# Linear layer, routed bias and first keys and values as one unrolled pipeline

## What is computed

```python
x = x + (layernorm(x) @ (weight * block_mask).T + bias)          # linear, block-sparse
h = layernorm(x)
scores = softmax(h @ router_weight.T + router_bias)              # 64 experts
top_w, top_i = top_k(scores, 8)
x = x + h * top_w.sum(-1) + dense(top_w, top_i) @ expert_bias    # routed bias
h = layernorm(x)
latent = concat(h @ Wk_down.T, h @ Wv_down.T)                    # 8 heads of 32 each
k, v = k_latent @ Wk_up.T, v_latent @ Wv_up.T                    # latent reshaped across tokens
# then causal attention with 32 query heads over 8 key heads, and a gated feed-forward of 1376
```

## Time and profile before

| | us |
|---|---|
| median of 3 runs | 1753.33 (1752.32 to 1753.48) |
| span of the profiled execution (its own time outside the span is not shown) | 1755.8 |
| PE busy | 1697.3 (97%) |
| DVE busy | 873.7 (50%) |
| ACT busy | 778.8 (44%) |
| POOL busy | 298.6 (17%) |

### The profile page before, as it was taken

The page is one execution under the profiler, slowest core; times in us unless marked ns, Lnnn a source line. Parts: engine busy times, 40 slices in busy tenths (PEclk is TensorE's granted clock), DMA queues, the critical chain, the costliest instruction groups (busy, mean ns, idle before and its releaser), DMA issues. The chain is left out here.

```text
span 1755.8 us, 27483 instructions
## 1 busy us (share of the span) xinstructions
PE 1697.3 (97%) x8546; PEld 1429.9 (81%) x8546; DVE 873.7 (50%) x2683; ACT 778.8 (44%) x2143; POOL 298.6 (17%) x669
## 2 busy tenths in 40 slices
PE   5788999999999999999999999999999899999999
PEld 4667897788888888888888888888888788888887
DVE  7776010555555555555656556556566553323212
ACT  4476434555455455445445536545545432121111
POOL 4611000121131122122113113112222000000000
PEclk9879999999999999999999999999999999999999
DMA  5200325111111101101101101100100231000000
GB/s 159 70 1 1 150 75 220 37 25 37 37 25 37 37 17 44 37 12 48 37 12 48 38 12 36 39 23 16 45 13 19 77 97 43 1 24 0 24 0 24
DMA packets 46996, 74.42 MB, mean 42 GB/s; under 512 B 4576, under 2 KB 23008, under 8 KB 44832
## 3 DMA queue, kind: packets, MB, share of 16 engines
q1 hardware_dynamic: 45984, 72.63, 12.9%
q10 hardware_dynamic: 896, 0.56, 0.1%
HBM read 52.20 MB, written 20.97 MB: 42 GB/s over the span
## 5 line engine op out<-in xcount | busy, mean ns | idle before, releaser
L963 POOL TENSOR_SCALAR prob<-prob,inv_sum 128x128 f32<-128x128 f32 x256 | 98.5, 385 | 829.5 <-DVE inv_sum L1106 829.5
L1201 PE MATMUL ps_q<-h_hi,kv_w_hi 128*128 128x512 f32 x512 | 205.9, 402 | 1.4 <-PEq L758 1.4
L991 ACT ACTIVATE prob<-prob,neg_max 128x128 f32<-128x128 f32 x256 | 100.6, 393 | 238.5 <-DVE neg_max L1101 238.5
L1201 PE MATMUL ps_q<-h_lo,kv_w_hi 128*128 128x512 f32 x512 | 200.3, 391 | 0.0
L1201 PE MATMUL ps_q<-h_hi,kv_w_lo 128*128 128x512 f32 x512 | 200.0, 391 | 0.0
L133 ACT ACTIVATE prob_t_hi<-ps_s 128x512 fp32r<-128x512 f32 x192 | 107.4, 598 | 73.3 <-PE ps_s L1250 73.3
L964 POOL TENSOR_SCALAR prob<-prob,inv_sum 128x256 f32<-128x256 f32 x256 | 136.9, 535 | 0.0
L1086 DVE TENSOR_TENSOR x<-ps_q,x 128x512 f32<-128x512 f32 x128 | 88.2, 689 | 96.7 <-PE ps_q L1279 96.7
L138 DVE TENSOR_TENSOR prob_t_lo<-ps_s,prob_t_hi 128x512 fp32r<-128x512 f32 x192 | 126.2, 685 | 15.1 <-ACT prob_t_hi L133 12.5
L993 ACT ACTIVATE prob<-prob,neg_max 128x256 f32<-128x256 f32 x256 | 127.1, 497 | 0.0
L1470 DVE SCALAR_TENSOR_TENSOR f_act<-f_ps_r,f_scale,f_act 128x512 f32<-128x512 f32 x44 | 33.0, 751 | 185.5 <-PE f_ps_r L1501 184.1
(11 more groups left out here) (184 smaller groups left out, 4251.4 us busy)
## 6 DMA issues: line engine op xcount, KB each, us to landing
k_scratch<-kv_stage SPq DMA_DIRECT2D x32, 256.0 KB, 2.4
v_scratch<-kv_stage SPq DMA_DIRECT2D x32, 256.0 KB, 2.0
w_raw<-in_wq_g SPq DMA_DIRECT2D x8, 1024.0 KB, 4.8
k_raw<-k_scratch SPq DMA_DIRECT2D x32, 256.0 KB, 3.4
v_raw<-v_scratch SPq DMA_DIRECT2D x32, 256.0 KB, 3.8
w_raw<-in_wo_g SPq DMA_DIRECT2D x8, 1024.0 KB, 5.9
x<-in_x SPq DMA_DIRECT2D x16, 256.0 KB, 2.9
out<-x SPq DMA_DIRECT2D x16, 256.0 KB, 2.1
```

The lines of the kernel that those rows point to most:

```text
L963: pool.tensor_scalar(prob[:, b, h, 0:P], prob[:, b, h, 0:P], inv_sum[:, b, h, 0:1], 1.0, ALU.mult, ALU.mult)
L991: act.activation(prob[:, b, h, 0:P], prob[:, b, h, 0:P], ACT.Exp, scale=-1.0, bias=neg_max[:, b, h, 0:1], accum_out=row_sum[:, b, h, 0:1])
L1201: last = pe.matmul(ps_q[:, h % 2, :], wq[a][:, c, h * HEAD:(h + 1) * HEAD], h3[b][:, c, pair * PAIR:(pair + 1) * PAIR], start=(c == 0 and ...
```

## The change

`block_sparse_linear`, `RouterWeights`, `RoutedBias`, `routed_bias_and_keys`, `skewed` are replaced by one function `head` with one block. All engines run the same unrolled sequence of slots i from -3 to 26; tile i is in the linear stage, and tile j = i - 8 in routing. 48 tasks stand in the slots 18 to 26, at three places of a slot, by the table `KV_PLACES`; the other 48 follow. A routing tile now takes four slots (j, j - 1, j - 2, j - 3) instead of ten iterations, with single buffers for h1, h1t and h2. DVE keeps two instructions of a norm (bn_stats, bn_aggr); POOL has three. The low part of the weight pieces and the scaling of x in routing go to POOL. Loads: the mask is first on SP's queue, the linear weight on ACT's; the wait for a weight piece's buffer is now on POOL's work.

```diff
-def skewed(eng, depth, body, first=None, tail=None):
-    for i in range(first):
-        body(i, i % 2, lambda k, i=i: i - k >= 0)
-    with eng.Fori(first // 2, TILES // 2) as j:
-        for par in range(2):
-            body(2 * j + par, par, lambda k: True)
-    for i in range(TILES, TILES + depth):
-        body(i, i % 2, lambda k, i=i: i - k < TILES)
-        if tail:
-            tail(i - TILES)
...
+class TileNorm:
+    def stats(self, dve, src, t):
+        dve.bn_stats(self.bn[:, t % 2, :], src).then_inc(self.bn_done, 1)
+        dve.wait_ge(self.bn_done, t + 1)
+        dve.bn_aggr(self.mv[:, t, :], self.bn[:, t % 2, :]).then_inc(self.mv_done, 1)
+    def power(self, pool, t):
+        pool.wait_ge(self.mv_done, t + 1)
+        pool.tensor_scalar(self.ve[:, t:t + 1], self.mv[:, t, 1:2], EPS, 1.0, ALU.add, ALU.mult).then_inc(self.ve_done, 1)
+        pool.wait_ge(self.ve_done, t + 1)
+        pool.tensor_tensor(self.factors[:, t, 0:1], self.ve[:, t:t + 1], self.half, ALU.pow).then_inc(self.rstd_done, 1)
+        pool.wait_ge(self.rstd_done, t + 1)
+        pool.tensor_scalar(self.factors[:, t, 1:2], self.mv[:, t, 0:1], self.factors[:, t, 0:1], -1.0, ALU.mult, ALU.mult).then_inc(self.factors_done, 1)
+    def activate(self, act, out, src, t):
+        act.wait_ge(self.factors_done, t + 1)
+        return act.activation(out, src, ACT.Identity, bias=self.factors[:, t, 1:2], scale=self.factors[:, t, 0:1])
...
-                block_sparse_linear(nc, sem, sb, ps, split, x, ident, half, consts, ln[0], ln[1], x_in, mask_t, w0_t, bias0,
-                                    lambda eng: router.load(eng, router_t, router_bias, expert_bias), kv_weights, kv_w)
-                stored = routed_bias_and_keys(nc, sem, sb, ps, split, x, ident, ln[1], ln[2], router, h3, kv_w, stream, wq_g, k_scr, v_scr)
+            stored = head(nc, sem, sb, ps, split, x, ident, half, consts, ln, h3, kv_w, stream, x_in, mask_t, w0_t, bias0,
+                          router_t, router_bias, expert_bias, kv_weights, wq_g, k_scr, v_scr)
...
+LAG = TILES // 2
+SLOTS = TILES + LAG + 3
+KV_PLACES = {18: (0, 0, 2), 19: (1, 1, 2), 20: (2, 1, 3), 21: (2, 1, 3), 22: (2, 2, 2), 23: (2, 2, 2),
+             24: (2, 2, 2), 25: (2, 2, 2), 26: (2, 2, 2)}
...
+        early = sb("early", [P, 2 * KC * HID], F32, st)
+        h1, h1t, h2 = [early[:, n * HID:(n + 1) * HID] for n in range(3)]
+        chosen, chosen_t = [early[:, 3 * HID + 2 * n * P:3 * HID + 2 * (n + 1) * P].rearrange("p (a n) -> p a n", a=2) for n in range(2)]
+        stage = [w_raw[:, n, :] for n in range(STAGES)]
+        ps_t0, ps_y0 = bank[:, 0:2, :], bank[:, 2:4, :]
+        ps_t1, ps_l, ps_m, ps_n = [bank[:, n, :] for n in range(4, 8)]
+        ps_c = ps_l[:, P:2 * P]
...
+                for c in range(KC):
+                    sp.dma_start(mask[:, c, :], mask_t[c * P:(c + 1) * P, :]).then_inc(mask_loaded[c], 16)
+                for t in range(TILES):
+                    if t >= 4:
+                        sp.wait_ge(x_loaded[t % 4], 16 * (t // 4))
+                    sp.dma_start(x[:, t, :], x_in[t * P:(t + 1) * P, :]).then_inc(x_loaded[t % 4], 16)
+                    if t >= 3:
+                        piece = t - 3
+                        if piece >= 2:
+                            sp.wait_ge(kv_lo, piece - 1)
+                        sp.dma_start(kv_raw[:, piece % 2, :], kv_weights[piece, :, :]).then_inc(kv_loaded[piece % 2], 16)
...
+                def split_piece(n):
+                    pool.wait_ge(kv_hi, n + 1)
+                    lo_part(pool, [w[:, n, :] for w in kv_w], kv_raw[:, n % 2, :]).then_inc(kv_lo, 1)
+                for i in range(-3, SLOTS):
+                    j = i - LAG
+                    if i == 0:
+                        pool.wait_ge(rows_done, KC)
+                        pool.memset(chosen[:, :, EXPERTS:P], 0.0).then_inc(padded, 1)
+                    if in_a(j - 3):
+                        ln[2].power(pool, j - 3)
+                    if in_a(j - 2):
+                        t = j - 2
+                        pool.wait_ge(combined_done, t + 1)
+                        pool.tensor_scalar(x[:, t, :], x[:, t, :], combined[:, t % 2, 0:1], combined[:, t % 2, 1:2],
+                                           ALU.mult, ALU.add).then_inc(scaled_done, 1)
+                    if in_a(i + 3):
+                        ln[0].power(pool, i + 3)
+                    if in_a(i + 2):
+                        t = i + 2
+                        if t == 0:
+                            pool.wait_ge(bias_loaded, 16)
+                        pool.wait_ge(h0_done, t + 1)
+                        pool.tensor_tensor(x[:, t, :], x[:, t, :], bias[:, :], ALU.add).then_inc(xb_done, 1)
+                    if in_a(i):
+                        ln[1].power(pool, i)
+                        split_piece(i)
+            @block.scalar
...
+                for c in range(KC):
+                    act.dma_start(w_raw[:, c, :], w0_t[c * P:(c + 1) * P, :]).then_inc(w_loaded[c], 16)
...
+                for i in range(-3, SLOTS):
+                    j = i - LAG
+                    if i == -1:
+                        weight_hi(0)
+                        weight_hi(1)
+                    if in_a(i + 1):
+                        hi0(i + 1)
+                    if i in places:
+                        for n in places[i][0]:
+                            task(n)
+                    if in_a(i + 2):
+                        normal0(i + 2)
+                    if i == -1:
+                        weight_hi(2)
+                        weight_hi(3)
+                    if in_a(j - 1):
+                        exponentials(j - 1)
+                    if in_a(j):
+                        normal1(j)
+                    if in_a(j - 3):
+                        normal2(j - 3)
+                    if in_a(j - 2):
+                        chosen_copy(j - 2)
+                    if in_a(i):
+                        piece_hi(i)
+                    if i in places:
+                        for n in places[i][1]:
+                            task(n)
+                    if in_a(j):
+                        flipped_copy(j)
+                    if in_a(j - 3):
+                        hi2(j - 3)
+                    if i in places:
+                        for n in places[i][2]:
+                            task(n)
+                for n in range(mixed, len(tasks)):
+                    task(n)
...
+                for i in range(-3, SLOTS):
+                    j = i - LAG
+                    if in_a(j - 3):
+                        stats2(j - 3)
+                    if in_a(j - 1):
+                        biased(j - 1)
+                    if in_a(i + 1):
+                        lo0(i + 1)
+                    if in_a(i + 3):
+                        stats0(i + 3)
+                    if i in places:
+                        for n in places[i][0]:
+                            task(n)
+                    if in_a(j - 1):
+                        choose(j - 1)
+                    if in_a(i):
+                        add(i)
+                    if i in places:
+                        for n in places[i][1]:
+                            task(n)
+                    if in_a(j - 2):
+                        mixed_in(j - 2)
+                    if in_a(j - 3):
+                        lo2(j - 3)
+                    if i in places:
+                        for n in places[i][2]:
+                            task(n)
+                for n in range(mixed, len(tasks)):
+                    task(n)
...
+                    if n == 0:
+                        pe.wait_ge(kv_lo, TILES)
...
+                for i in range(-3, SLOTS):
+                    j = i - LAG
+                    if in_a(i + 1):
+                        flip0(i + 1)
+                    if in_a(j - 1):
+                        score(j - 1)
+                    if i in places:
+                        for n in places[i][0]:
+                            task(n)
+                    if in_a(i):
+                        linear(i)
+                    if in_a(j):
+                        flip1(j)
+                    if in_a(j - 2):
+                        flip_chosen(j - 2)
+                    if i in places:
+                        for n in places[i][1]:
+                            task(n)
+                    if in_a(j - 3):
+                        flip2(j - 3)
+                    if in_a(j - 2):
+                        mix(j - 2)
+                    if i in places:
+                        for n in places[i][2]:
+                            task(n)
+                for n in range(mixed, len(tasks)):
+                    task(n)
```

More of the change, by code:

```diff
@@ L165, in build @@
         consts = sem("consts")
[L166 removed]
+        ln = [TileNorm(sb, sem, f"ln{n}", half[:, 0:1]) for n in range(3)]
+        ln_feed = LayerNorm(sb, sem, "ln3", half[:, 0:1], consts)
         h3 = split("h3", [P, KC, TOKENS])
[L169 removed]
```

(63 more changed lines are left out.)

631 lines of the change are left out of this document (222 added, 409 removed).

## The result

| | before | changed |
|---|---|---|
| median of 9 runs each, side by side | 1754.86 (1752.32 to 1761.21) | 1762.98 (1760.66 to 1765.84) |
| ratio, 95% interval | | 1.0047 (1.0035 to 1.0059) |
| span of the profiled execution | 1755.8 | 1761.2 |
| first latent task | 143.32 | 129.52 |
| attention starts | 299.07 | 303.62 |

The change is slower by 0.47%, where I forecast 1746.7 us, a gain. The first latent task does start earlier, and attention later. The spans differ by 5.4 us and the medians by 8.1: the changed kernel's profiled execution is its median (1762.98, 1.8 outside the span), while by the same 1.8 that of before took 1757.6, 2.7 above its median.

The account below looks back on a forecast made before the run. PE sets the end from 143 us, before that the chain through DVE, ACT and GpSimd. First task at 120.5 + 141.6 + 17.3 + 11.5 = 290.9 against 297.5: gain 6.6 from the median 1753.33, 1746.7 us; range 1735 to 1761.

Parts of the forecast that it names:

- The start: Loads, mask and weight work before slot 0: tile 0 added at 22 us, GpSimd's slot 0 ending at about 26.0.
- Slots 0 to 9: Linear stage: GpSimd sets the pace at 4.3 us a slot (two norms, bias add, piece), slot 9 ending at 64.7 us.
- Slots 10 and 11: Routing's entry: slot 10 takes 5.1 us with GpSimd's scale of x, then the first third norm's walk 3.3, to 73.1.
- Slots 12 to 15: Linear and routing together: DVE sets the pace, 6.9 + 6.5 + 6.5 + 6.3 = 26.2 us, to 99.3.
- Slots 16 to 18: Routing alone: one tile's chain per slot, TensorE at 1.2 GHz, 6.5, 7.2 and 7.5 us; first latent task at 120.5.
- The tasks: From slot 18 PE sets the end: 141.6 us of tasks, 17.3 of routing, 11.5 of gaps and clock, ending at 290.9.
- The five gaps: Slots 19 to 23: PE waits for ACT's norm, behind task evictions, before its flip; 2.0 us five times, 10 in all.
- The clock's return: In the task slots: 1.5 us added for TensorE's clock coming back.
- From there to the median: End of tasks to run time: attention and feed-forward unchanged, median 2.5 us under the profiled span, gain 6.6, 1746.7 us.
- the one through GpSimd: Rival, slower: GpSimd's slot 5.1 us, plus 0.8 of DVE contention in each of slots 9 to 18; 1763 us; chance 0.20.
- The rival of no change: Gain before the first task 3 to 6 us smaller, by TensorE at 1.2 GHz in slots 0 to 9; 1753; chance 0.20.
- the bounds for being wrong: GpSimd's pitch over 5, first latent task after 127 us, or PE's gaps before its flips summing to over 18 us.

Follow-up runs that it names:

- e3: The change with the addition of epsilon to the variance back on DVE for all norms, one GpSimd operation per norm less; 1756.91 us, ratio 1.0006 to the kernel before.
- e9: The change with GpSimd's subtraction for the low half of each weight piece done twice; 1776.2 us, ratio 1.0126 to the kernel before.
- e8: The change with eight needless 128x512 matmuls on TensorE in each of slots 16 to 18; 1756.97 us, ratio 1.0015 to the kernel before.
- e2: The change with only ACT's order altered: exponentials and first norm of a slot ahead of the first place's evictions; 1754.2 us, ratio 0.9993 to the kernel before.
- e1: The change with the low half of the 16 weight pieces back on DVE, at the slot's end; 1761.49 us, ratio 1.0037 to the kernel before.
- e12: The change with the pieces' low half back on DVE, a slot later and near the slot's beginning; 1757.55 us, ratio 1.0007 to the kernel before.

## Why the prediction was wrong

By its steps, against the trace of the change; the end of the tasks, reckoned as in the forecast (the last matmul's start and 0.26), is 302.0 us where I had 290.9.

- **The start** (22, 26.0): tile 0 was added at 23.43 and GpSimd's slot 0 ended at 27.4; 1.4 late. The masks were summed earlier than I took. The first w_lo, beside a bias add, took 1.70 us where the others take 0.66 to 0.69, and the bias add of tile 1, beside another w_lo, 1.81 and not 1.27; my sum had neither.
- **Slots 0 to 9: the step that failed.** "Sum 2.04 + 1.3 + 0.97 = 4.3 us" measured 4.75, and nine of them are 4.1 us, the largest of the misses. GpSimd as the limit, with no idle time, was right, and e3 and e9 show that the first task follows it. Only the size of the terms was off. The terms were too small by 0.25 for the two norms, 0.14 for the piece and 0.05 for the bias add. Part of it was to be read beforehand: I took durations (1.29) where the rows have start to start (1.38, from 36.44 to 37.82), and scaled the piece from the former. That the added small operation costs 0.40 and not 0.26 no row of before showed; e3 does (0.27 of the 0.44). Most of the rest is the power and the shift of the two norms, 0.88 each in e3 where before had 0.76: the shift is another instruction now, 0.26 long and not 0.19. The Trainium skill, page GPSIMD Engine Reference, section 4.1 (Engine selection), which I had cited and not followed, has GpSimd about 2x slower on two inputs. The trace agrees: 1.02 against 0.517 us is 1.97.
- **Slots 10 and 11** (8.4 us): 10.6. The scale of x took 0.76 to 0.83 us, no more than assumed; slot 10 is 5.6 and not 5.1 by the 0.45 of every GpSimd slot. The first third norm's walk took 5.0 us (75.82 to 80.82) instead of 3.3. The high part was done at 79.40, 3.6 after the walk's start, but VectorE, whose order has the add of the mixture first and which waited for PE's mixture until 79.47, took the low part only at 80.14: I had left that add out.
- **Slots 12 to 15** (26.2 us): 26.0. DVE's count held.
- **Slots 16 to 18** (21.2 us): 22.6, the chain and the low clock as told. e8 shows what I had not drawn from it: 4.3 us of it are the clock's and can be had back.
- **The tasks** (170.4 us with gaps): 172.5 between the first task and the end. The five gaps have the place, the number and the releaser forecast, 1.72 us of waiting each where I had 2.0 with reaction, 8.6 in all for my 10; e2 shows that they are paid. The clock's return, a term of 1.5 for which I gave no row, cost 1.4 (eight matmuls at the low level from 129.52). So 3.6 us are more work on TensorE than I took over from before. The second half of the batch has 0.9 of them (71.7 us from 230.32, where before had 70.8 for the same matmuls); why is open.
- **From there to the median.** 11.1 us late at the end of the tasks, 0.9 more behind it, and 4.2 because the profiled execution that I set out from lay 2.7 above the median, and the 9 runs' median 1.5 above that of the three: together 16.2 of the 16.3 us.

Of the rivals, the one through GpSimd named the time, 1763, and the engine. Its conditions were not met as written: the pitch is 4.75 and not 5.1, and its second half, 0.8 us of contention in each of ten slots, measured 4.0 in all, 2.7 of it in slots 11 to 18 (in nine of slots 9 to 18 one of the three small operations that it names took 0.46 to 1.02 us in place of 0.15 to 0.22). So it had the right engine, and its time by luck. The rival of no change wanted TensorE at 1.2 GHz through slots 0 to 9; the granted clock there was 0.96. Of the bounds for being wrong, "after 127" was crossed by the first task (129.52), the two others not.

The balance in one line: the first task came 13.8 us earlier and the tasks took 18.3 longer than before (172.5 against 154.2), of which 16.2 were forecast. The gain rested on a difference of two large terms, 22.8 less 16.2. GpSimd's slot alone, 4.1 us, would have left 2.5 of the 6.6; misses of 1 to 2 us in four other steps, all to the same side, turned the sign.

Not tried: the linear layer and routing in their old stages with only the small norm operations moved. So what the interleaving alone is worth in the old kernel stays open.

## What to carry to other kernels

Where an engine is to set the pace of a pipeline, cost its slot by start to start in the rows, add a semaphore's worth to every small operation (0.4 us here for a row of 0.19), and multiply by the number of slots. In an order written by hand look, for each engine that is half idle, at what stands ahead of the one instruction that the full engine waits for: moving three lines gave 8.8 us. And choose the distance between interleaved stages so that few slots are left in which a single tile's chain runs alone: each lasted 7.2 to 7.7 us here, 1.1 to 1.6 of them by TensorE's lower clock, and taking two away brought the first task 11.0 us forward.

## What the runs showed of the hardware

A VectorE subtraction with both inputs in SBUF took 0.517 us alone, 0.53 to 1.51 us when it began 0.1 us or more before the end of a GpSimd two-input operation of 1.3, and then ended 0.40 to 0.43 us after it, in the kernel before, in e1 and in e12; one with an input in PSUM was not touched (0.66). Placing it a little later within the GpSimd operation therefore costs less, though the end stays the same. Eight needless matmuls a slot, 2.1 us of them, held TensorE's granted clock at 1.00, its 2.4 GHz level, where it had been 0.64 over the same stretch (107.0 to 125.2 us), and shortened every slot by more than a microsecond.
